# One operation for a row tile of the attention product, another place for the quantisation's low part and scales, and layer norm moments of two pairs on another engine

## The reference

```
xn = (x - mean(x)) / sqrt(var(x) + 1e-5)

Q, K, V = xn @ Wq.T + bq, xn @ Wk.T + bk, xn @ Wv.T + bv
Q, K = Q / norm(Q, axis=tokens), K / norm(K, axis=tokens)
tailor = 1 / (L + Q . (sum(K) + 1e-6))
s = xn + gamma * (sum(V) + Q (K^T V)) * tailor

def fp4(x):                       # blocks of 16 along the last axis
    scale = max(max|block| / 6, 1e-12)
    return nearest(x / scale, {0, .5, 1, 1.5, 2, 3, 4, 6}) * scale

gate, up = fp4(xn) @ fp4(w_gate).T, fp4(xn) @ fp4(w_up).T     # 256 -> 704
f = fp4(silu(gate) * up) @ fp4(w_down).T                       # 704 -> 256
out = x + s * silu(f)
```

## Time and profile before

| | |
|---|---|
| median of 3 runs | 592.88 us (592.57 to 593.26) |
| profiled execution, its own time | 593.2 us |
| span of the profile | 591.5 us |
| PE busy | 547.5 us (93%), 4973 matmuls |
| DVE busy | 554.6 us (94%), 1180 instructions |
| ACT busy | 415.6 us (70%), 902 instructions |
| POOL busy | 243.4 us (41%), 213 instructions |
| mean granted clock of PE | 0.987 |

### The profile page before, as it was taken

The page is one execution under the profiler, slowest core; times in us unless marked ns, Lnnn a source line. Parts: engine busy times, 40 slices in busy tenths (PEclk is TensorE's granted clock), DMA queues, the critical chain, the costliest instruction groups (busy, mean ns, idle before and its releaser), DMA issues. The chain is left out here.

```text
span 591.5 us, 15211 instructions
## 1 busy us (share of the span) xinstructions
PE 547.5 (93%) x4973; PEld 424.9 (72%) x4973; DVE 554.6 (94%) x1180; ACT 415.6 (70%) x902; POOL 243.4 (41%) x213
## 2 busy tenths in 40 slices
PE   0478999999999999999999989999999999999996
PEld 0356777778787777778787767778787777778875
DVE  6998999999999999999999997999999999987783
ACT  4979888877787787767676766777776777555431
POOL 6524433333434434434443343444343344422146
PEclk9969899999999999999999999999999999999999
DMA  8010000000011001111011111110111101103124
GB/s 253 18 37 19 19 20 19 19 20 19 19 37 37 19 2 57 55 55 55 33 44 36 54 58 56 55 36 27 49 54 55 56 37 38 37 33 129 37 95 174
DMA packets 17633, 29.15 MB, mean 49 GB/s; under 512 B 2704, under 2 KB 5136, under 8 KB 17552
## 3 DMA queue, kind: packets, MB, share of 16 engines
q1 hardware_dynamic: 17552, 28.13, 14.3%
HBM read 19.73 MB, written 8.39 MB: 48 GB/s over the span
## 5 line engine op out<-in xcount | busy, mean ns | idle before, releaser
L1495 PE MATMUL GU<-wgu,xqT 128*128 128x352 f16 x1536 | 253.7, 316 | 3.6 <-issue 2.3
L1495 PEld LDWEIGHTS GU<-wgu,xqT 128*128 128x128 f16 x1536 | 148.5, 99 | 78.2 <-issue 3.4
L564 POOL TENSOR_TENSOR ht<-h,hrr 128x1408 f32<-128x1408 f32 x32 | 82.9, 2589 | 80.2 <-DVE hrr L992 78.7
L659 ACT ACTIVATE sil<-GU,wkap 128x352 f32<-128x352 f32 x128 | 70.7, 552 | 55.7 <-PE GU L1495 54.8
L1505 PE MATMUL DS<-wdT,hqT 128*128 128x256 f16 x704 | 87.3, 272 | 0.6 <-ACT hqT L666 0.6
L523 POOL TENSOR_TENSOR xnat<-xs,xnat 128x510 f16<-128x510 f32 (+1 forms) x32 | 37.0, 1157 | 106.1 <-DVE hq L1026 89.7
L1026 DVE TENSOR_TENSOR hq<-hg,hs 128x704 f16<-128x704 f16 x128 | 79.1, 658 | 1.0
L978 DVE SCALAR_TENSOR_TENSOR h<-GU,wkap,sil 128x352 f32<-128x352 f32 x128 | 68.7, 537 | 11.6 <-ACT sil L659 8.0
L1505 PEld LDWEIGHTS DS<-wdT,hqT 128*128 128x128 f16 x704 | 66.8, 98 | 10.4 <-ACT hqT L666 0.9
L513 POOL TENSOR_TENSOR rs<-ve,half 128x2 f32<-128x2 f32 x32 | 23.8, 744 | 110.0 <-DVE ht L1015 106.1
L695 ACT ACTIVATE gring<-DS,hun 128x256 f32<-128x256 f32 (+1 forms) x64 | 29.8, 465 | 42.9 <-issue 29.1
(11 more groups left out here) (176 smaller groups left out, 954.9 us busy)
## 6 DMA issues: line engine op xcount, KB each, us to landing
xin<-in_L_attn_x SPq DMA_DIRECT2D x34, 256.0 KB, 2.8
xe<-in_L_attn_x SPq DMA_DIRECT2D x24, 256.0 KB, 2.8
out<-o SPq DMA_DIRECT2D x24, 256.0 KB, 2.0
algebra<-in_L_ffn_w_down SPq DMA_DIRECT2D x1, 704.0 KB, 7.3
gring<-in_L_ffn_w_up SPq DMA_DIRECT2D x1, 640.0 KB, 6.1
xs<-in_L_attn_x SPq DMA_DIRECT2D x2, 256.0 KB, 4.2
xt<-in_L_attn_x SPq DMA_DIRECT2D x2, 256.0 KB, 4.8
out<-xin SPq DMA_DIRECT2D x2, 256.0 KB, 2.0
```

The costliest lines, as they stand in the source:

```text
L564: g.tensor_tensor(paired(ht[:, 0:2 * I]), paired(h[:, q]), spread(hrr[:, q], 4 * CB), ALU.mult).then_inc(S["ht_d"], 1)
L659: a.activation(sil[:, c], GU[:, c, 0, 0:CH], ACT.Silu, scale=wkap[:, 0:1]).then_inc(S["sil_d"], 1)
L1495: last = t.matmul(GU[:, c, m, 0:CH], xqT[:, k, j, 2 * a_ + kc], wgu[:, b_, kc, 2 * m + c], start=(z == 0 and kc == 0), stop=(z == 2 and kc ...
```

## The change

**One operation for y.** `e_row` makes the whole y of a tile, 256 columns, reading both halves from the two PSUM banks, in place of two `e_half`. It stands behind h of half 1 of its tile. gate_up of a tile waits, before its half 0 only, for the whole y of the tile before. At the first tile with attention product of each batch (last_halves), the two halves stay.

**Low part.** x_low on POOL no longer waits for the hq of tile 0 of pair p-1 (hloq, 2p-1) but for hg of that pair (hg_d, p).

**Order on DVE.** All x_scales parts and part 2 of `parts` come before x_round 0 and 1. h of (1,1) and y of tile 1 come before all four hq.

**Moments on ScalarE.** For pairs 1 and 4 the mean and the variance are no longer made by bn_stats and bn_aggr on DVE, but by four passes over 256 columns on ACT with accumulated sums (`x_moments`), into the tiles o and xe, which are not in use yet. dve_pairs counts the rest.

```diff
+        def dve_pairs(u):
+            if isinstance(u, int):
+                return 2 * (u + 1 - (u > 1) - (u > 4))
+            return 2 * u - 2
...
-                        wait(pool, "hloq", 2 * p - 1)
+                        wait(pool, "hg_d", p)
                        x_low(p, k)
...
                 u = p + LEADA
                 wait(act, "nb_d", u)
-                wait(act, "aggr", 2 * u + 2)
+                wait(act, "aggr", dve_pairs(u))
                 a.activation(nm[:, :], mv[:, :, 0], ACT.Copy, scale=-1.0).then_inc(S["var_m"], 1)
                 a.activation(ve[:, :], mv[:, :, 1], ACT.Copy, bias=EPS_LN / XSCALE ** 2, scale=1.0 / XSCALE ** 2).then_inc(S["var_e"], 1)
+            def x_moments(p, k, to):
+                u, q = p + LEADA, (k + LEADA) % 2
+                act.wait_ge(S[f"x_in{q}"], 8 * (u - q) + 16)
+                wait(act, "nb_d", u)
+                for j in range(2):
+                    a.activation(to[:, j, 0:D], xin[:, q, j], ACT.Copy, scale=-1.0 / D, accum_out=nm[:, j:j + 1]).then_inc(S["var_m" if j else "mean_0"], 1)
+                for j in range(2):
+                    act.wait_ge(*((S["var_m"], u + 1) if j else (S["mean_0"], 1 + (u > 1))))
+                    a.activation(to[:, j, D:2 * D], xin[:, q, j], ACT.Square, bias=nm[:, j:j + 1], accum_out=squares[:, j:j + 1]).then_inc(S["moments"], 1)
+                act.wait_ge(S["moments"], 2 + 2 * (u > 1))
+                a.activation(ve[:, :], squares[:, :], ACT.Copy, bias=EPS_LN / XSCALE ** 2, scale=1.0 / (D * XSCALE ** 2)).then_inc(S["var_e"], 1)
...
             x_norm(-3, 1)
+            x_moments(-2, 0, o)
             w_abs(0)
             x_high(-3, 1)
             x_abs(-2, 0)
-            x_stats(-2)
...
                 rows_out(-1, 1, j, False, False)
+            x_moments(1, 1, xe)
...
-                if on["xf"]:
+                if on["xf"] and not (isinstance(p, int) and p == 0):
                     x_stats(p + 1)
...
+            def e_row(p, k, j):
+                e, q, row = s_place(p, k, j)
+                halves = lambda ap: ap.rearrange("p (c n) -> p c n", c=2)
+                wait(dve, "s_d", 4 * e + 2 * row + 2)
+                wait(dve, "g_d", 2 * e + row + 1)
+                if row == 0:
+                    wait(dve, "o_d", e - 1)
+                v.scalar_tensor_tensor(halves(y[:, q, row * D:(row + 1) * D]), GU[:, :, 1, CH:CH + P], unm[:, 0:1],
+                                       halves(ring(gring, e, GRING)[:, row]), ALU.mult, ALU.mult).then_inc(S["y_d"], 2)
...
             w_scales(1, 2)
-            x_front(-2, 0)
-            x_spread(1)
...
-            dve.wait_ge(S["aggr"], 6)
+            dve.wait_ge(S["aggr"], 4)
...
                 if on["m"]:
                     h_mul(p, k, 0, 0, i)
-                if s_beside(p, 0, tail):
-                    e_half(p, k, 0, 0, last_halves(0, i))
                 if s_beside(p, 0, tail) and last_halves(0, i):
+                    e_half(p, k, 0, 0, True)
                     e_half(p, k, 0, 1, True)
                 attention(0, 0)
-                if on["xf"]:
+                own = on["xf"] and not (isinstance(p, int) and p == 0)
+                if own:
                     x_front(p + 1, 1 - k)
                 attention(0, 5)
-                if on["xf"]:
-                    wait(dve, "stats", 2 * (p + LEADA + 1) + 2)
+                if own:
+                    wait(dve, "stats", dve_pairs(p + LEADA + 1))
                     wait(dve, "var_e", p + LEADA + 1)
                 if on["mb"]:
                     parts(p, k, 0)
-                if on["xf"]:
+                if own:
                     x_var()
                 if on["mb"]:
                     parts(p, k, 1)
...
                 if on["m"]:
                     h_mul(p, k, 0, 1, i)
                 if s_beside(p, 0, tail) and not last_halves(0, i):
-                    e_half(p, k, 0, 1)
+                    e_row(p, k, 0)
                 attention(0, 4)
                 if on["e"] and not on["m"]:
                     e_mul(p, k, 0)
                 if on["xa"]:
                     x_scales(p, k, 0)
                 attention(0, 2)
-                if on["xb"]:
-                    x_round(p, k, 0)
-                    x_round(p, k, 1)
-                if on["mb"]:
-                    parts(p, k, 2)
                 if on["xa"]:
                     x_scales(p, k, 1)
                 if on["xb"]:
                     x_scales(p - 1, 1 - k, 3)
+                if on["xa"]:
+                    x_scales(p, k, 2)
+                if on["mb"]:
+                    parts(p, k, 2)
+                if on["xb"]:
+                    x_round(p, k, 0)
+                    x_round(p, k, 1)
                 attention(0, 3)
                 if on["mb"]:
                     h_round(p, k, 0)
-                if on["xa"]:
-                    x_scales(p, k, 2)
                 if on["m"]:
                     h_mul(p, k, 1, 0, i)
-                if s_beside(p, 1, tail):
-                    e_half(p, k, 1, 0)
                 if on["xb"]:
                     x_round(p, k, 2)
                 if on["mb"]:
                     h_round(p, k, 1)
+                if on["m"]:
+                    h_mul(p, k, 1, 1, i)
+                if s_beside(p, 1, tail):
+                    e_row(p, k, 1)
                 attention(1, 0)
                 if on["mb"]:
                     h_round(p, k, 2)
-                if on["m"]:
-                    h_mul(p, k, 1, 1, i)
-                if s_beside(p, 1, tail):
-                    e_half(p, k, 1, 1)
                 attention(1, 1)
                 if on["mb"]:
                     h_round(p, k, 3)
...
                 wait(pe, "h_d", n - 1)
-                if s_on:
-                    wait(pe, "y_d", n - 4 * LAGE - 3 + ((i, j, c) == (FIRST, 1, 0)))
+                if s_on and c == 0:
+                    wait(pe, "y_d", 4 * (p - LAGE) - 2 + 2 * j)
                 if s_on and c == 0 and last_halves(j, i):
                     s_half(p, k, j, 1, b, i)
```

5 lines of the change are left out of this document (3 added, 2 removed).

## The result

The changed kernel takes 594.0 us (median of 14 runs, 592.28 to 595.68) against 592.58 before (14 runs): a ratio of 1.0019, 95% interval 1.0012 to 1.0026. That is 1.1 us slower by the ratio (1.4 by the two medians), clear of the noise but far from 2%. The forecast was 593.3 in 588.5 to 597.0.

The account below looks back on a forecast made before the run. DVE was taken to pace most pairs, PE pairs 7 to 9, 30 and 31. Terms -0.3 + 2.3 - 3.4 + 1.4 + 0.4 = +0.4 gave 593.6 us profiled, 593.3 as median; range 588.5 to 597.

Parts of the forecast that it names:

- The new y row: One DVE operation per tile costs 0.40 us instead of 0.52 for two halves; at most 4.9 us of DVE saved.
- The first hq beside the low part: First hq loses 0.49 instead of 0.65 (0.16 won); 0.65 won with turn or product between; 0.25 worse without y.
- Small steps are held by the port: POOL's add holds the first two-input scale step instead of xt; the loss only moves, gain taken as 0.
- Head: Moments of pairs 1 and 4 on ScalarE give -0.5, the collision in pair 1 +0.2: -0.3 us together.
- Pairs 10 to 13, 18 to 21, 26 and 27: DVE keeps the pace and each pair wins the plain 0.40 (0.24 from y, 0.16 from hq); together -3.4 us.
- Pairs 2 to 9: Later hq of tile 0 and norms 1.4 later at pair 7, with PE pacing pairs 8 and 9: +2.3 us.
- Pairs 14 to 17 and 22 to 25: Win nothing: the wait on y delays PE, and DVE's 2 us saved become waits for sil.
- Pairs 28 to 31 and the end: PE tied to 4.6 ahead paces the end, +1.4 us; last pair's ham later by +0.4 us.
- The signs: DVE busy about 5 us less, sil waits some 15; wrong if pairs 22-25 shorten over 1 us or pair 10 isn't later.
- The third: Rival: PE's first product of each tile, behind the y row, sets the pace; pairs 10 to 27 win nothing; 596.7 us, 23%.
- The fourth: Rival: POOL's low part costs hq 0.9 even with y in front; DVE-paced pairs give back 0.4 each; 595.5 us, 12%.

Follow-up runs that it names:

- e5: Kernel before with only h of (1,1) and its y half moved ahead of the first two hq: 590.03 us, ratio 0.9961.
- e3: Changed kernel with mean and variance of pairs 1 and 4 on VectorE again: 593.72 us, ratio 1.0019.
- e9: Changed kernel with the scale steps behind xt and xg again: 592.62 us, ratio 0.9998.
- e8: Changed kernel with the y row ahead of h of half 1 and, for tile 1, the attention step ahead of both: 588.90 us, ratio 0.9938.
- e6: Kernel before with only y of a tile in one operation and gate_up waiting for the whole row: 596.27 us, ratio 1.0057.
- e10: Kernel before with h and y of (1,1) ahead of the first two hq and GpSimd's low part behind hg: 595.24 us, ratio 1.0036.
- e4: Changed kernel with GpSimd's low part released by the hq of tile 0 again: 597.54 us, ratio 1.0084.
- e12: Kernel before with attention step, one-operation y, then h of (1,1) ahead of four hq, and gate_up waiting for the whole row: 586.43 us, ratio 0.9895.
- e11: Kernel before with the attention step, then h and y of (1,1), ahead of the first two hq: 587.55 us, ratio 0.9917.
- e1: Changed kernel with y in two halves again, gate_up of each half waiting only for its own y half: 599.35 us, ratio 1.0112.
- e2: Changed kernel with the y row ahead of h of half 1 instead of behind it: 593.24 us, ratio 1.0010.

## Why the prediction was right, and where it was not

The time came out at 594.0 for a forecast of 593.3, and the sum within the profiled executions (+0.4) at +0.1. That the sum fits so well is luck: half of its terms came out as forecast, the others were off by 1 to 2 us, one way and the other. The terms are compared by VectorE's first h of each pair, as the second table has them.

*The new y row*: 0.40 for a tile forecast, 0.39 measured. *The first hq beside the low part*: a loss of 0.49 forecast, 0.52 to 0.53 in the plain pairs (1.03 against 0.51), 0.30 in pairs 10, 11 and 28, none where an attention step stands in between. In pairs 1 to 5 and 8, without y, it is 0.69 as in the third hq before, and not 0.90: the low part starts there 0.08 behind hg and not 0.30. Slow first hq are 20 and not 28.

*Small steps are held by the port*: right in what came of it; seven xss were long, up to 1.24. But the forecast named the first step with two inputs, and that is xs, which keeps its 0.18. The step that was held, xss, has one tensor as input and two constants, and so has hss, which was held in e5, while ham, with one input too, keeps its 1.6. The rule for two inputs, on which the forecast went, doesn't cover them. The same section of the Trainium skill (SBUF — State Buffer, Who interferes with whom) has tensor_scalar among the operations that can take the shared port pair in a two-port mode, and tensor_reduce as one that never contends on trn2. With that this trace agrees: xss and hss are the one, ham is the other.

*Head*, -0.3: VectorE's first h of pair 2 is 0.2 earlier; the first gate_up of all is 0.47 earlier, but at TensorE's start of pair 2 nothing of it is left, and e3 shows no gain.

*Pairs 10 to 13, 18 to 21, 26 and 27*, "win the plain 0.40", -3.4 together: -3.6. The waits for the row at pairs 11, 19 and 27 took nothing from that. But they stand elsewhere than forecast (pairs 20, 26 and 27). I had taken only TensorE's attention work as what uses up the play between a y row and the next h. At pairs 10, 18 and 26 the opposite holds: VectorE has the last steps of the attention matrix (Mx) to do, TensorE has none left, comes early, and waits 0.9 to 1.4 for the row. What TensorE loses there is the distance by which it runs ahead.

*Pairs 2 to 9*, +2.3 forecast: +1.0. The squares and norms of pair 7 came late as described. The wait at the norms, before and after:

```profile
151.75 1.05 PE L1599 MATMUL G<-ones,wqkv 128*128 128x1 f32 x8 [0.20 <-DVE algebra L1093]
153.24 1.05 PE L1627 MATMUL G<-ones,wqkv 128*128 128x1 f32 x8 [1.22 <-DVE algebra L1125]
```

TensorE's start of pair 10 is 2.0 later by it, but VectorE's first h of that pair only 0.8, since TensorE was 5.2 ahead there and is 4.0 ahead now.

*Pairs 14 to 17 and 22 to 25*, "win nothing", 0 forecast: they lost 0.7 and 1.3. This is the term that was furthest off. VectorE didn't wait for sil there before; in the changed kernel it waits 3.0 us in pairs 14 to 17 and 3.6 in pairs 22 to 25, and not the 2 of the forecast, and most of the loss stands at the first h behind the norms, of pairs 16 and 24 (1.0 each). In pairs 22 to 25 the clock has a part as well: in e9, where it stays up at pair 20, they take 69.53 us instead of 70.54. With the step that the norms wait for moved ahead (e8) both groups take 68.25, a microsecond less than before the change.

*Pairs 28 to 31 and the end*, +1.8 forecast: +1.9 to the end of the last operation. TensorE is 4.5 ahead of VectorE at pair 28 (4.6 forecast, 6.9 before), and its waits for VectorE, 0.9 in the forecast, are gone: its three steps from pair 28 to 31 are 0.9 shorter together. What no part of the forecast held is the last transfer, which lands 1.0 sooner. Without it the changed kernel would have come out at some +1.1 instead of +0.1.

*The signs.* h(23,0,1) comes right behind sil, as foretold (at 410.60, after 1.23 of waiting); pair 10 starts 2.0 later. TensorE's steps from pair 22 to 26 are shorter by 0.7, under the 1 us set as a limit. VectorE lost 11.5 us of busy time and not 5: some 5 are y, 0.9 the moments (544.0 in e3, where they are back), and the rest is what is left of the hq's collisions with the low part, which cost 10.7 instead of 18.9, after small losses elsewhere. It waits 20.5 for sil and not 15. The norms' wait ahead of pair 24 is 0.88, not longer than 0.92; the one ahead of pair 8 did grow.

*The rivals.* The third (y wait makes PE the bound) named the mechanism. It has pairs 10 to 27 winning nothing, the forecast 3.4; they won 1.6, half-way. It put the play in the wrong place. The fourth (a loss of 0.9 at the first hq) is out with the 0.52.

What no part of the prediction held: that the move of h and y ahead of the hq is the one that wins, of the two that were run alone (e5, e6), and that where GpSimd's low part falls decides over it. I had looked at the early low part as a small gain (0.16); on this order it costs 4 to 5 us (e5 to e10). VectorE's busy time is the same in both, so what costs is not how much collides but what: in e10 the squares, and behind them the norms and TensorE's clock. With the row the sign is the other way (e4 to the changed kernel, -3.5). With row and step ahead it seems to turn again: e12, with the late low part, is faster than e8 with the early one (ratios 0.9895 and 0.9938, intervals apart), but these two differ in scale steps and moments too, and in the last transfer. So the parts do not add. Low part and scale steps were never run alone on the kernel before. Why the late low part breaks into the four hq in 15 pairs of e4, in 7 of e5, 5 of e11 and 3 of e12 is not settled.

*The median.* Of the changed kernel's 14 runs the four with a granted clock of 1.000 over the span took 592.28 to 593.16, the ten with 0.990 to 0.997 took 593.27 to 595.68. The 23 runs of the kernel before beside e1 to e4 go from 0.987 to 0.999 and from 592.17 to 593.61 with no such order. So at full clock the changed kernel takes what the kernel before takes, and the 1.1 us of the ratio go with drops of the clock. That waits which the change gave TensorE cause these drops is not shown. The one trace of the changed kernel has its drop at pair 20, behind the idle time that all kernels have there. The wait at the norms of pair 7 did grow, from 0.20 to 1.22, and in e2 a drop follows it; but in the traces of the changed kernel, e1, e3, e9 and e10 none does behind the same 1.2 us. No run took the waits away and left all else.

## What to carry to other kernels

When two engines are both over 90% busy, the work taken off one is worth something only where the other doesn't then wait for a later step of it: count each new wait against the places where the waited-for engine has extra work, not only where the waiting one has. Where two engines share a port, look at who is put to waiting: a short run of operations back to back, with the rival released inside it, cost this kernel less than a rival released early (e5 against e10). It was the other way with the row in the kernel (e4), so such an order has to be tried together with the rest. And let a step for whose result the other engine stands idle go ahead of steps that it needs later (e8, e11: 3.4 and 2.0 us in three steps). Count a lead that an engine loses apart from time that the whole loses: here TensorE's first gate_up was 1.0 to 3.4 us later than before in pairs 8 to 30, while VectorE's first h was earlier in most of the pairs from 13 on. And look at the end of the trace, where a transfer's landing can hide or feign a microsecond.
